# First attention of a two-layer perceiver: values weighed after every fourth step instead of after every second, and after the scores of those same steps

## The chip, the cores and the metric

The kernel runs on one core of one Trainium2 chip. The metric is the device time of one execution in microseconds (us), and of several executions the median. Engines: PE is TensorE (its weight loads are listed apart, as PEld), DVE is VectorE, ACT is ScalarE, POOL is GpSimd, SP is SyncE, which here only issues transfers.

## The reference, cut to what matters

The program is two layers of a perceiver: cross attention over a long context, a convolution mixer, a quantised feed-forward, a second cross attention, a self attention and a mixture of experts. The change touches the first cross attention alone:

```
B, S, S2, E, H = 2, 256, 4096, 256, 16;  D = E // H
q = proj(layernorm(x), Wq, bq)          # 2 x 16 heads x 256 queries x 16
k = proj(ctx, Wk, bk); v = proj(ctx, Wv, bv)   # 2 x 16 heads x 4096 keys x 16
energy = q @ k^T / sqrt(D);  energy = where(mask == 0, -1e9, energy)
attn = softmax(energy)                  # over 4096 keys
x = x + (attn @ v) @ Wo^T + bo
```

In the inputs used no entry of the mask is zero, so the kernel takes the branch without masks.

## The kernel before, in words

The attention works on 8 **groups** (`gg`, 2 batches x 4 groups of 4 heads), and each group has 32 **steps** (`KC`, 128 keys each). Two sorts of score matmuls are made of the same keys and queries:

- **Direct scores**, `scores(n)`: queries on the partitions, 2 matmuls of 512 keys each into two PSUM banks. They serve only to find the row maximum: DVE reduces the two banks (`row_tops`, L951). A unit `n` may be written once unit `n-2` is reduced (`pe.wait_ge(s_maxed, n - 1)`, L1493), since there are two pairs of banks. They run 38 units ahead of the steps (`UNITS + AHEAD`), so that they stand beside steps 0 to 217 and no longer beside steps 218 to 255.
- **Turned scores**, `turned_scores(step)`: keys on the partitions, 4 matmuls of 256 queries in two pairs. The row maximum is already taken off through extra rows of the operands. Each pair fills one bank of a **ring of 3 banks**; ACT turns it into exponentials in one of 4 buffers `PR` (`exps`, L684) and so empties it. A slot of the ring may be filled once the slot three places earlier has been emptied (`ring_free`, L1465). The order of all users of the ring is written out in `ring_slots`.
- **Weighing**, `weigh_values(step)`: 4 products of the values (32 columns each, side by side in the array) with the exponentials of the step, accumulated in the bank `PV`. They are f32, and each stands as two matmuls in the trace, 8 in a step. The buffer of a step is free for the exponentials of the fourth step after it once `pv_done` has counted it.

What else goes through the ring: in groups 0 and 1 the key projections of the second batch (`project_keys`, one piece every four steps, followed by two ACT copies, a DVE split and a POOL subtraction), in group 3 its value projections (`project_values`), the row maxima of the next group (`turn_max`), and the turning of a finished group's result (`turn_context`). Nothing is scheduled by a planner: the order on each engine is the order of the loops, and PE, ACT and DVE each have their own copy of it.

Before the change PE's loop goes over pairs of steps: turned and direct scores of the pair `m`, then the weighing of the pair `m-1`. ACT so has a whole pair's time for its exponentials before PE asks for them. At the start of a group the weighing that stands behind the first pair is still that of the group before.

Of the kernel before, what the change touches and what calls it, by code (L numbers as in the profile page):

```python
# [24 lines left out]
KC = S2 // P  # L25
# [30 lines left out]
GROUPS = B * (H // 4)  # L56
QUARTERS = 4
UNITS = 8 * QUARTERS
# [22 lines left out]

def ring_slots():

    turn = itertools.count()
# [9 lines left out]
    for gg in range(GROUPS):  # L94
        for m in range(KC // 2):
            if m == KC // 2 - 1 and gg + 1 < GROUPS:
                for pair in range(2):
                    tops[gg + 1, pair] = next(turn)
            for step in (KC * gg + 2 * m, KC * gg + 2 * m + 1):
                for pair in range(2):  # L100
                    exps[step, pair] = next(turn)
            if gg < 2 and m % 2:
                keys[1, 4 * gg + m // 4, m // 2 % 2] = next(turn)
            if gg and m == 1:
                contexts[gg - 1] = next(turn)
            if (gg == 3 and m) or (gg == 4 and m == 0):
                done = KC // 2 * (gg - 3) + m - 1
                values[1, done // 2, done % 2] = next(turn)
# [5 lines left out]


def values_after(gg, m):

    if (gg == 3 and m) or (gg == 4 and m == 0):
        return divmod(KC // 2 * (gg - 3) + m - 1, 2)
    return None  # L120


def keys_at(gg, m):

    if gg < 2 and m % 2:
        return 4 * gg + m // 4, m // 2 % 2
    return None


def build(nc, t):  # L130

    ctx = ExitStack()
    with ctx:
# [495 lines left out]
        def _(act):  # L629
# [78 lines left out]
            for gg in range(GROUPS):  # L708
                for m in range(KC // 2):
                    if m == KC // 2 - 1 and gg + 1 < GROUPS:  # L710
                        copy_tops(gg + 1)
                    exps(KC * gg + 2 * m)
                    exps(KC * gg + 2 * m + 1)
                    if keys_at(gg, m):
                        copy_keys(1, *keys_at(gg, m))
                    if gg and m == 1:
                        copy_context(gg - 1)
                    if gg and m == 0:
                        copy_weighed(gg - 1)
                    if values_after(gg, m):  # L720
                        copy_values(1, *values_after(gg, m))
# [174 lines left out]
        def _(dve):  # L896
# [150 lines left out]
            for step in range(GROUPS * KC):  # L1047
# [398 lines left out]
        def _(pe):  # L1446
# [114 lines left out]
            def attend(masked):  # L1561
# [13 lines left out]
                for gg in range(GROUPS):  # L1575
                    for m in range(KC // 2):
                        if m == KC // 2 - 1 and gg + 1 < GROUPS:
                            turn_max(gg + 1)
                        for step in (KC * gg + 2 * m, KC * gg + 2 * m + 1):
# [3 lines left out]
                        if keys_at(gg, m):  # L1583
                            project_keys(1, *keys_at(gg, m))
                        if gg and m == 1:
# [4 lines left out]
                        if values_after(gg, m):  # L1590
                            project_values(1, *values_after(gg, m))
                        if gg + 1 == GROUPS and m == KC // 4:
# [4 lines left out]
                weigh_values(GROUPS * KC - 2)  # L1597
                weigh_values(GROUPS * KC - 1)
# [471 lines left out]
```

## Time and profile before

| | |
|---|---|
| median of 3 runs | 1069.17 us (1062.98 to 1069.81) |
| the profiled execution | 1063.51 us, its span 1061.6 us |
| busy in it | PE 922.1 us (87%), DVE 601.9 us (57%), ACT 479.4 us (45%), POOL 76.2 us (7%) |
| first attention's steps | from 146.9 to 574.1 us of the span |

Shares of busy time are means over stages with different limits. The median is 5.7 us above the profiled execution; what surrounds the span is 1.9 us.

### The profile page before, as it was taken

The page shows a single profiled execution, that of the slowest core. Times are in us where ns is not written, and L with a number is a line of the kernel's source. Part 1 is how long each engine was busy: PE and PEld are TensorE (multiplying, and loading weights), DVE is VectorE, ACT ScalarE, POOL GpSimd, SP SyncE. Part 2 cuts the span into 40 slices and gives each one's busy share as a digit, 9 for nine tenths or more (in the row PEclk, how much of TensorE's full clock was granted, in tenths as well). Part 3 has the DMA queues.
Part 4 walks back from the last instruction along what each step waited for, and adds up shares of the span by engine and source line. Part 5 has one row for each costly group of instructions (what it writes and reads, how often), then busy time and mean ns, then how long its engine had stood idle before and what let it go on. Part 6 is the DMA issues. An engine that isn't in the chain of part 4 may idle for free.

```text
span 1061.6 us, 14994 instructions
## 1 busy us (share of the span) xinstructions
PE 922.1 (87%) x5928; PEld 527.9 (50%) x5928; DVE 601.9 (57%) x1064; ACT 479.4 (45%) x939; POOL 76.2 (7%) x85
## 2 busy tenths in 40 slices
PE   4367889999999999999988896249999989999878
PEld 2134544444545655555445354034656764566656
DVE  1366887778885448888723845872332227288340
ACT  1222257777775457777786330421310210677201
POOL 0131101111000000000002000300000006100000
PEclk9778999999999999999998999669999989999979
DMA  9846874665635224436235206013634450000000
GB/s 313 158 115 153 155 172 123 131 159 133 123 60 100 31 41 68 72 61 142 81 115 214 79 1 237 0 58 141 213 144 160 158 159 0 1 1 1 1 0 21
DMA packets 65555, 108.67 MB, mean 102 GB/s; under 512 B 6854, under 2 KB 40390, under 8 KB 63302
## 3 DMA queue, kind: packets, MB, share of 16 engines
q1 hardware_dynamic: 63276, 100.35, 37.0%
q10 hardware_dynamic: 2208, 7.34, 2.0%
q8 instruction: 49, 0.80, 0.4%
q14 instruction: 22, 0.18, 0.1%
HBM read 93.77 MB, written 13.89 MB: 101 GB/s over the span
## 4 chain that ended last, share of the span: by engine, by line
PE 76%; DVE 9%; ACT 6%; DMA 5%; issue 3%; SPq 1%; POOL 0%; ACTq 0%; DVEq 0%
PE psum L1547 12%; PE psum L1529 10%; PE psum L1500 9%; PE psum L1820 5%; PE psum L1791 5%; PE psum L1484 5%; PE psum L1644 4%; PE psum L1850 4%; PE psum L1474 4%; PE psum L1657 4%; PE psum L1882 3%; ACT arena L684 2%; DMA arena<-rows 2%; DMA kparts<-arena 2%; PE psum L1896 2%
## 5 line engine op out<-in xcount | busy, mean ns | idle before, releaser
L951 DVE TENSOR_REDUCE arena<-psum 128x1 f32<-128x1024 f32 x256 | 301.3, 1219 | 113.2 <-PE psum L1500 113.2
L684 ACT ACTIVATE arena<-psum 128x512 f32<-128x512 f32 x512 | 264.2, 605 | 58.5 <-PE psum L1529 57.4
L1529 PE MATMUL psum<-arena 99*128 99x256 bf16 x1024 | 160.5, 274 | 9.2 <-ACT arena L684 5.4
L1500 PE MATMUL psum<-arena 96*128 96x512 bf16 x512 | 150.6, 379 | 6.5 <-DVE arena L951 4.2
L1547 PE MATMUL psum<-arena 128*32 128x256 f32 x2048 | 136.8, 385 | 0.0
L1529 PEld LDWEIGHTS psum<-arena 99*128 99x128 bf16 x1024 | 79.3, 97 | 107.9 <-ACT arena L684 52.9
L1547 PEld LDWEIGHTS psum<-arena 128*32 128x32 f32 x2048 | 53.5, 109 | 75.4 <-ACT arena L684 36.9
L1474 PE MATMUL psum<-arena 128*128 128x512 f32 x128 | 65.5, 643 | 27.3 <-ACT arena L662 18.1
L1484 PE MATMUL psum<-arena 128*128 128x256 f32 x256 | 62.2, 385 | 0.0
L661 ACT ACTIVATE arena<-psum,arena 128x512 bf16<-128x512 f32 x32 | 22.0, 688 | 86.6 <-PE psum L1474 49.3
L1500 PEld LDWEIGHTS psum<-arena 96*128 96x128 bf16 x512 | 49.4, 98 | 23.4 <-DVE arena L951 9.1
L1820 PE MATMUL psum<-arena 128*128 128x256 f32 x256 | 55.9, 379 | 0.0
L1791 PE MATMUL psum<-arena 128*128 128x512 f32 x128 | 55.5, 593 | 0.0
L591 POOL TENSOR_TENSOR arena<-arena 128x512 bf16<-128x512 f32 x32 | 38.8, 1213 | 231.6 <-DVE arena L937 231.6
L1484 PEld LDWEIGHTS psum<-arena 128*128 128x128 f32 x256 | 47.3, 189 | 14.6 <-issue 7.5
L1474 PEld LDWEIGHTS psum<-arena 128*128 128x128 f32 x128 | 24.8, 205 | 55.7 <-issue 54.8
L1820 PEld LDWEIGHTS psum<-arena 128*128 128x128 f32 x256 | 48.3, 190 | 6.4
L667 ACT ACTIVATE arena<-psum 128x512 f32<-128x512 f32 x32 | 19.1, 597 | 67.0 <-PE psum L1484 67.0
L1644 PE MATMUL psum<-arena 128*128 128x512 f32 (+1 forms) x112 | 44.1, 551 | 3.3 <-ACT arena L743 0.9
L839 ACT ACTIVATE arena<-psum 128x512 f32<-128x512 f32 x16 | 9.6, 597 | 78.5 <-PE psum L1807 78.5
L1850 PE MATMUL psum<-arena 128*128 128x512 f32 x96 | 43.2, 610 | 0.7 <-ACT arena L741 0.7
L1258 DVE CUSTOM_DVE_ANT_0 arena<-psum,arena 128x512 f32<-128x512 f32 x32 | 22.1, 692 | 32.9 <-PE psum L1791 30.7
(231 smaller groups left out, 990.0 us busy)
## 6 DMA issues: line engine op xcount, KB each, us to landing
arena<-kparts SPq DMA_DIRECT2D x192, 128.0 KB, 5.3
kparts<-arena SPq DMA_DIRECT2D x32, 384.0 KB, 4.3
arena<-ctxT SPq DMA_DIRECT2D x18, 512.0 KB, 5.6
arena<-ctxT SPq DMA_DIRECT2D x2, 4096.0 KB, 12.8
arena<-ctx SPq DMA_DIRECT2D x2, 4096.0 KB, 14.6
arena<-mask SPq DMA_DIRECT2D x8, 1024.0 KB, 6.7
arena<-mask ACTq DMA_DIRECT2D x4, 1024.0 KB, 15.5
arena<-w1e SPq DMA_DIRECT2D x2, 2048.0 KB, 10.3
```

Source lines behind the costliest of these rows:

```text
L684: nc.scalar.activation(PR[step % 4][:, pair * CH:(pair + 1) * CH], ring_bank(slot), ACT.Exp)\
L951: nc.vector.tensor_reduce(MX[g % 2][:, col:col + 1], unit_banks(n).rearrange("p b n -> p (b n)"), AX.X, ALU.max).then_inc(s_maxed, 1)
L1474: last = nc.tensor.matmul(ring_bank(slot), WK[:, k, f * P:(f + 1) * P], CTX[n % SLOTS][:, k, :], start=(k == 0), stop=(k == CT - 1))
L1484: last = nc.tensor.matmul(ring_bank(slot)[:, v * 256:(v + 1) * 256], CTX[n % SLOTS][:, k, (2 * i + v) * P:(2 * i + v + 1) * P], WV[:, k, : ...
L1500: last = nc.tensor.matmul(out, q, KST[g % 2][0:ROWS, j, at], start=True, stop=not masked, skip_group_check=True)
L1529: last = nc.tensor.matmul(ring_heads(slot)[:, u, :], KST[gg % 2][0:KROWS, j, kc * P:(kc + 1) * P], QST[0:KROWS, G * g + j, b * S:(b + 1) * S],
L1547: last = nc.tensor.matmul(PV[32 * j:32 * (j + 1), :], V_flat[:, at:at + 32], PR[step % 4][:, j * S:(j + 1) * S], start=(kc == 0), stop=(kc ...
L1644: last = nc.tensor.matmul(out, weights[:, k, m * P:m * P + width], xs[k], start=(k == 0), stop=(k == n - 1))
L1657: last = nc.tensor.matmul(out, lhs[k], weights[:, k, :], start=(k == 0 and not biased), stop=(k == n - 1), skip_group_check=biased)
L1791: last = nc.tensor.matmul(psum[:, n % 4, :], QC[:, c, w * P:(w + 1) * P], CTXT[w // 2][:, c, n * 512:(n + 1) * 512], start=(c == 0), stop= ...
L1820: last = nc.tensor.matmul(psum[:, 6, 0:256], PT1[:, k * P:(k + 1) * P], CTXK[w // 2][:, k, :], start=(k == 0), stop=(k == KC - 1))
L1850: last = nc.tensor.matmul(psum[:, bank, :], HTF[:, c, i * P:(i + 1) * P], WQKV[which][:, c, half * HALF:(half + 1) * HALF], start=(c == 0) ...
```

## The change

PE's loop goes over runs of four steps. The turned and direct scores of the four steps come first, then the weighing of those same four steps. One piece of the key projections stands in each run of groups 0 and 1, between scores and weighing; it was in every second pair. The value projections come two pieces at a time, after the weighing of each run of group 3; before there was one in each pair, ending in group 4. The row maxima of the next group are turned at the start of its last run (step 28, before: step 30). The result of a group is copied by ACT ahead of the first exponentials of the next group, and turned after the first four steps' scores. After the last step nothing is left to weigh. ACT and DVE follow the same order; the key split of a piece stands on DVE behind the second reduction of the next run. No instruction is added or removed, no buffer, bank or ring slot is added.

```diff
+RUN = 4
+RUNS = KC // RUN
+def steps_of(gg, m):
+    return range(KC * gg + RUN * m, KC * gg + RUN * (m + 1))
...
@@ ACT
-                for m in range(KC // 2):
-                    if m == KC // 2 - 1 and gg + 1 < GROUPS:
+                for m in range(RUNS):
+                    if m == RUNS - 1 and gg + 1 < GROUPS:
                         copy_tops(gg + 1)
-                    exps(KC * gg + 2 * m)
-                    exps(KC * gg + 2 * m + 1)
...
                     if gg and m == 0:
                         copy_weighed(gg - 1)
+                    for step in steps_of(gg, m):
+                        exps(step)
+                    if gg < 2:
+                        copy_keys(1, 4 * gg + m // 2, m % 2)
+                    if gg and m == 0:
+                        copy_context(gg - 1)
+                    if gg == 3:
+                        for i in range(2):
+                            copy_values(1, m, i)
@@ DVE
-                if k % 2 == 1 and step >= 3:
-                    before = divmod(step // 2 - 1, KC // 2)
-                    if keys_at(*before):
-                        split_keys(1, *keys_at(*before))
+                if k % RUN == 1 and 0 < step // RUN <= 2 * RUNS:
+                    piece = step // RUN - 1
+                    split_keys(1, piece // 2, piece % 2)
@@ PE
-                        for step in (KC * gg + 2 * m, KC * gg + 2 * m + 1):
+                        for step in steps_of(gg, m):
                             turned_scores(step, masked)
                             if step + UNITS + AHEAD < GROUPS * UNITS:
                                 scores(step + UNITS + AHEAD, masked)
-                        if keys_at(gg, m):
-                            project_keys(1, *keys_at(gg, m))
-                        if gg and m == 1:
+                        if gg < 2:
+                            project_keys(1, 4 * gg + m // 2, m % 2)
+                        if gg and m == 0:
                             turn_context(gg - 1)
-                        if gg or m:
-                            weigh_values(KC * gg + 2 * m - 2)
-                            weigh_values(KC * gg + 2 * m - 1)
-                        if values_after(gg, m):
-                            project_values(1, *values_after(gg, m))
+                        for step in steps_of(gg, m):
+                            weigh_values(step)
+                        if gg == 3:
+                            for i in range(2):
+                                project_values(1, m, i)
...
-                weigh_values(GROUPS * KC - 2)
-                weigh_values(GROUPS * KC - 1)
                 turn_context(GROUPS - 1)
```

**PE, two pairs of steps in a middle group, before.** L1529 is turned scores, L1500 direct scores, L1547 weighing.

```order
L1529 MATMUL psum<-arena 128x256 x4
L1500 MATMUL psum<-arena 128x512 x2
L1529 MATMUL psum<-arena 128x256 x4
L1500 MATMUL psum<-arena 128x512 x2
L1547 MATMUL psum<-arena 32x256 x8
L1529 MATMUL psum<-arena 128x256 x4
L1500 MATMUL psum<-arena 128x512 x2
L1529 MATMUL psum<-arena 128x256 x4
L1500 MATMUL psum<-arena 128x512 x2
L1547 MATMUL psum<-arena 32x256 x8
```

**The same four steps after the change.** Here L1522 is turned scores, L1493 direct scores, L1540 weighing.

```order
L1522 MATMUL psum<-arena 128x256 x4
L1493 MATMUL psum<-arena 128x512 x2
L1522 MATMUL psum<-arena 128x256 x4
L1493 MATMUL psum<-arena 128x512 x2
L1522 MATMUL psum<-arena 128x256 x4
L1493 MATMUL psum<-arena 128x512 x2
L1522 MATMUL psum<-arena 128x256 x4
L1493 MATMUL psum<-arena 128x512 x2
L1540 MATMUL psum<-arena 32x256 x16
```

Four units of direct scores now follow one another without a weighing between the second and the third, and the weighings of two pairs have become one block.

**PE after the change, from step 216, where the direct scores end.** L1507 is the turning of the row maxima for group 7.

```order
L1493 MATMUL psum<-arena 128x512 x2
L1522 MATMUL psum<-arena 128x256 x4
L1493 MATMUL psum<-arena 128x512 x2
L1522 MATMUL psum<-arena 128x256 x8
L1540 MATMUL psum<-arena 32x256 x16
L1507 MATMUL psum<-arena 3x128 x8
L1522 MATMUL psum<-arena 128x256 x16
L1540 MATMUL psum<-arena 32x256 x16
```

Without direct scores between them, the turned scores of four steps, eight slots of the ring, now stand in one piece; before there were four slots and then a weighing.

**PE in group 3, before**, a pair of steps with its value projection (L1484).

```order
L1529 MATMUL psum<-arena 128x256 x4
L1500 MATMUL psum<-arena 128x512 x2
L1547 MATMUL psum<-arena 32x256 x8
L1484 MATMUL psum<-arena 128x256 x4
L1529 MATMUL psum<-arena 128x256 x4
```

After the change the weighing of 16 is followed by a value projection of 8 in a row, once in four steps.

## Rows read from the trace of the kernel before

**Rows 1.** The page: the chain that ended last, by engine.

```profile
PE 76%; DVE 9%; ACT 6%; DMA 5%; issue 3%; SPq 1%; POOL 0%; ACTq 0%; DVEq 0%
```

**Rows 2.** Timeline, one pair of group 4: start, duration in us, engine, line.

```profile
426.33 0.61 PE L1529 MATMUL psum<-arena 99*128 99x256 bf16 x4
...
426.76 2.06 ACT L684 ACTIVATE arena<-psum 128x512 f32<-128x512 f32 x4 [0.78 <-PE psum L1529]
426.77 0.60 PE L1500 MATMUL psum<-arena 96*128 96x512 bf16 x2
...
427.41 2.36 DVE L951 TENSOR_REDUCE arena<-psum 128x1 f32<-128x1024 f32 x2 [0.49 <-PE psum L1500]
...
427.65 0.60 PE L1500 MATMUL psum<-arena 96*128 96x512 bf16 x2
...
428.17 1.07 PE L1547 MATMUL psum<-arena 128*32 128x256 f32 x16
...
429.18 0.61 PE L1529 MATMUL psum<-arena 99*128 99x256 bf16 x4
```

**Rows 3.** Timeline, step 0: the one place with four steps unbroken.

```profile
148.17 4.03 ACT L684 ACTIVATE arena<-psum 128x512 f32<-128x512 f32 x8
...
149.69 3.49 DVE L951 TENSOR_REDUCE arena<-psum 128x1 f32<-128x1024 f32 x3 [0.47 <-PE psum L1500]
...
150.03 0.60 PE L1500 MATMUL psum<-arena 96*128 96x512 bf16 x2
...
151.01 0.60 PE L1500 MATMUL psum<-arena 96*128 96x512 bf16 x2
...
153.25 1.07 PE L1547 MATMUL psum<-arena 128*32 128x256 f32 x16
```

**Rows 4.** Chain ahead of the steps: direct scores held by a reduction.

```profile
120.16 1.23 DVE arena L951
...
121.44 0.60 PE psum L1500 x2
```

**Rows 5.** Timeline, the last two pairs of group 7, without direct scores.

```profile
570.68 0.83 PE L1529 MATMUL psum<-arena 99*128 99x256 bf16 x6
571.11 2.06 ACT L684 ACTIVATE arena<-psum 128x512 f32<-128x512 f32 x4 [0.34 <-PE psum L1529]
...
571.76 0.39 PE L1529 MATMUL psum<-arena 99*128 99x256 bf16 x2 [0.25 <-ACT arena L684]
...
572.08 1.93 PE L1547 MATMUL psum<-arena 128*32 128x256 f32 x32
```

**Rows 6.** Timeline, a pair of group 3 with a value projection (L1484).

```profile
337.01 0.60 PE L1529 MATMUL psum<-arena 99*128 99x256 bf16 x4
...
339.10 1.07 PE L1547 MATMUL psum<-arena 128*32 128x256 f32 x16
...
340.10 1.99 PE L1484 MATMUL psum<-arena 128*128 128x256 f32 x8
...
341.93 0.49 PE L1529 MATMUL psum<-arena 99*128 99x256 bf16 x3
```

**Rows 7.** Timeline, the last pair of group 4, from the turning of the maxima.

```profile
437.63 0.61 PE L1514 MATMUL psum<-arena 128*3 128x128 bf16 x8
...
438.17 0.92 PE L1529 MATMUL psum<-arena 99*128 99x256 bf16 x4
...
439.15 2.06 ACT L684 ACTIVATE arena<-psum 128x512 f32<-128x512 f32 x4
...
441.56 0.61 PE L1529 MATMUL psum<-arena 99*128 99x256 bf16 x4
```

**Rows 8.** Windows: length, busy us of PE, PEld, DVE, ACT, POOL; PEclk; DMA.

```profile
80.00:88.00 8.00, 2.64 (x3) 1.17 (x4) 0.00 (x0) 0.00 (x0) 0.00 (x0) 0.59 0.90 224
...
314.48:400.69 86.21, 84.50 (x649) 49.76 (x645) 44.24 (x45) 47.43 (x94) 0.00 (x0) 1.00 0.33 57
...
528.01:574.06 46.05, 41.17 (x464) 19.92 (x460) 12.89 (x13) 38.90 (x77) 0.00 (x0) 1.00 0.31 112
```

More of the change, by code:

```diff
@@ L94, in ring_slots @@
     for gg in range(GROUPS):
-        for m in range(KC // 2):
-            if m == KC // 2 - 1 and gg + 1 < GROUPS:
+        for m in range(RUNS):
+            if m == RUNS - 1 and gg + 1 < GROUPS:
                 for pair in range(2):
                     tops[gg + 1, pair] = next(turn)
-            for step in (KC * gg + 2 * m, KC * gg + 2 * m + 1):
+            for step in steps_of(gg, m):
                 for pair in range(2):
                     exps[step, pair] = next(turn)
-            if gg < 2 and m % 2:
-                keys[1, 4 * gg + m // 4, m // 2 % 2] = next(turn)
-            if gg and m == 1:
+            if gg < 2:
+                keys[1, 4 * gg + m // 2, m % 2] = next(turn)
+            if gg and m == 0:
                 contexts[gg - 1] = next(turn)
-            if (gg == 3 and m) or (gg == 4 and m == 0):
-                done = KC // 2 * (gg - 3) + m - 1
-                values[1, done // 2, done % 2] = next(turn)
+            if gg == 3:
+                for i in range(2):
+                    values[1, m, i] = next(turn)
     contexts[GROUPS - 1] = next(turn)
@@ L113 @@
 KEY_AT, VALUE_AT, EXP_AT, TOP_AT, CONTEXT_AT = ring_slots()
[L116 to L127, printed above, removed]
 def build(nc, t):
@@ L708, in _ @@
             for gg in range(GROUPS):
-                for m in range(KC // 2):
-                    if m == KC // 2 - 1 and gg + 1 < GROUPS:
+                for m in range(RUNS):
+                    if m == RUNS - 1 and gg + 1 < GROUPS:
                         copy_tops(gg + 1)
-                    exps(KC * gg + 2 * m)
-                    exps(KC * gg + 2 * m + 1)
-                    if keys_at(gg, m):
-                        copy_keys(1, *keys_at(gg, m))
-                    if gg and m == 1:
-                        copy_context(gg - 1)
                     if gg and m == 0:
                         copy_weighed(gg - 1)
-                    if values_after(gg, m):
-                        copy_values(1, *values_after(gg, m))
+                    for step in steps_of(gg, m):
[7 more added lines that the diff above has]
+                            copy_values(1, m, i)
             copy_weighed(GROUPS - 1)
@@ L1575, in attend @@
                 for gg in range(GROUPS):
-                    for m in range(KC // 2):
-                        if m == KC // 2 - 1 and gg + 1 < GROUPS:
+                    for m in range(RUNS):
+                        if m == RUNS - 1 and gg + 1 < GROUPS:
                             turn_max(gg + 1)
-                        for step in (KC * gg + 2 * m, KC * gg + 2 * m + 1):
+                        for step in steps_of(gg, m):
                             turned_scores(step, masked)
@@ L1582, in attend @@
                                 scores(step + UNITS + AHEAD, masked)
-                        if keys_at(gg, m):
-                            project_keys(1, *keys_at(gg, m))
-                        if gg and m == 1:
+                        if gg < 2:
+                            project_keys(1, 4 * gg + m // 2, m % 2)
+                        if gg and m == 0:
                             turn_context(gg - 1)
-                        if gg or m:
-                            weigh_values(KC * gg + 2 * m - 2)
-                            weigh_values(KC * gg + 2 * m - 1)
-                        if values_after(gg, m):
-                            project_values(1, *values_after(gg, m))
-                        if gg + 1 == GROUPS and m == KC // 4:
+                        for step in steps_of(gg, m):
+                            weigh_values(step)
+                        if gg == 3:
+                            for i in range(2):
+                                project_values(1, m, i)
+                        if gg + 1 == GROUPS and m == RUNS // 2:
                             pe.wait_ge(on["w_summed"], 2)
```

## The prediction

> **What bounds the kernel now.** I read the chain that ended last first: PE holds 76% of it [rows 1]. Then the timeline inside the attention, since only its order changes. In a plain pair (two steps, group 4) I count from its first turned scores at 426.33 [rows 2]: ACT starts its exponentials at +0.43, the direct scores of the two steps start at +0.44 and +1.32 (a step of turned and direct scores is 0.88), DVE starts the first reduction at +1.08, the weighing starts at +1.84, and the next pair at +2.85. No idle time stands before a matmul on PE: the pair is PE's. ACT works 2.06 of the 2.85 us and DVE 2.36; both wait for PE. The reader is to see two more things in these rows. First, PE's hand-overs: from the last direct scores to the weighing 0.52 us pass, where from direct scores to turned scores it is 0.44, and the weighing of two steps needs 1.01 us until the next matmul, though two more steps joined on to a block add only 0.86 (1.93 for 32 matmuls [rows 5] less 1.07 for 16 [rows 2]). Second, DVE's slack exists only because of the weighing: a reduction is 1.23 long [rows 4], a second one starts 1.14 after the first (2.36 for two [rows 2]), and that is more than the 0.88 in which PE makes a unit.
>
> **What the change removes.** Half of the hand-overs. A run of four steps without any wait has its last direct scores at 1.32 + 2 x 0.88 = 3.08, its weighing at 3.60, and the next run at 3.60 + 1.01 + 0.86 = 5.47, against 2 x 2.85 = 5.70: 0.23 us saved.
>
> **What it adds: DVE's wait.** Four units now follow one another with two pairs of banks. The first reduction runs from 1.08 to 2.30, the second from 2.22 to 3.44. PE wants to write the third unit at 0.44 + 2 x 0.88 = 2.20. A held unit starts 0.05 after the reduction that held it (120.16 + 1.23 = 121.39, start at 121.44 [rows 4]), so at 2.35. Turned scores follow at 2.79, and the fourth unit wants to start at 3.23 but is held until 3.44 + 0.05 = 3.49. Then the weighing is at 4.01 and the next run at 4.01 + 1.87 = 5.88, **+0.18 us a run against before**. The kernel before has one such place, step 0 to 3: units start at 150.03 and 151.01, 0.98 apart and not 0.88, and the latter just behind the end of the reduction begun at 149.69 [rows 3]. Queued behind the held direct scores are the next turned scores, for which ACT waits, and the weighing; nobody else is on the path. DVE starts the third and fourth reductions at 3.36 and 4.50 and ends at about 5.7, before the next run's second unit, so no debt is carried. In groups 0 and 1 the key split comes behind the second reduction, about 1.2 us, but the key projection gives the next run 1.7 us more. I cost it at nothing; without that cover it would hold the next run's first unit by under 1 us.
>
> **ACT and the ring in such a run.** Eight exponentials in a row take 4.03, that is one every 0.48, the last about 0.67 long [rows 3]. The eighth starts at 0.43 + 7 x 0.48 = 3.79 and ends near 4.46; its weighing, the fourth of the block, is due at 4.01 + 3 x 0.43 = 5.30. So following the same steps' scores costs no wait. The tightest slot is the eighth: its predecessor by three ends near 3.0, and PE is there at 2.79 + 0.22 = 3.01. It lies 0.2 us ahead of DVE's hold, which covers small delays. The four `PR` buffers are free, since the weighing of a run is over before the next run's first exponential.
>
> 39 runs are plain ones with four units (groups 0 to 6 without group 3, without the first run of groups 0 and 4, the last run of each group and the last two of group 6): 39 x 0.18 = **+7.0 us**.
>
> **Step 0.** Scores and keys as before up to the weighing at 153.25 [rows 3], then four steps weighed instead of two: **+0.9**.
>
> **The last runs of groups 0, 1, 2, 4, 5.** The turning of the maxima takes 0.54 up to the turned scores (437.63 to 438.17), and ACT begins the exponentials 0.98 behind these and not 0.43; the pair takes 3.39 [rows 7], 0.54 above a plain one. After, the same two delays fall on a run: following them through the ring the fourth unit starts at 3.80, the weighing at 4.32, in all 0.76 above 5.88, against 0.99 above 5.70 before: 5 x -0.05 = **-0.2**. Turning the context costs 0.22 in both.
>
> **Group 3.** A pair with values takes 4.92 (337.01 to 341.93) [rows 6]. The weighing starts at +2.09 and not +1.84, since ACT copies values ahead of the exponentials and the ring waits for it; the projection stands 1.00 behind the weighing and takes 1.83 to the next turned scores. After, ACT's lateness (0.25) disappears behind DVE's hold, and one hand-over falls away: 4.01 + 1.00 + 0.86 + 1.83 + 1.73 = 9.43 for four steps. Eight of them, the maxima (some 0.9), the context and the first run of group 4 (5.88 and its context) make 82.7, against 86.21 for the same stretch [rows 8]: **-3.5**.
>
> **Without direct scores.** A pair has its fourth slot held until the first exponential is over (571.76, +1.08), weighs at +1.40 and takes 1.40 + 1.01 = 2.41 [rows 5]. After, slots four to eight are each held, one every 0.49: the eighth fills at 1.08 + 4 x 0.49 = 3.04, the weighing is at 3.36, the run takes 5.23 against 4.82. Nine runs: 9 x 0.41 = +3.7. The run from step 216 gains 0.1, and at the end the block of four steps (1.93 [rows 5]), two of which are a debt of earlier pairs, is gone: -0.9. Together **+2.7**.
>
> **Sum:** 7.0 + 0.9 - 0.2 - 3.5 + 2.7 = **+6.9 us**. The profiled execution would go from 1063.5 to 1070.4. It is 5.7 below the median of its kernel, within the spread of the three runs (1062.98 to 1069.81); on the median the sum gives 1076. One per cent, 10.7 us, is about what a measurement of this kernel can tell from no change.
>
> What comes after the attention keeps its place relative to its end: the loads of weights wait for the weighing of group 6, now counted earlier before the end, and for the weights' quantisation, some 2 us later relative to the end but still over when it comes.
>
> **Rivals.** *No wait on DVE appears* (the reductions are quicker in a row, or PE's slack hides them): every one of the 54 runs with four units gains 0.42 on my sum, 6.9 - 22.7 = -16, **1053 us**. For it: every idle row of DVE before names PE. Against it: rows 3 show the hold with four steps in a row. 0.08.
>
> *The ring of three slots holds as well*: each held slot makes its exponentials later, and the fourth unit then waits for PE's own turned scores, not for DVE. The price is that of group 3, where late exponentials move the weighing by 0.25 [rows 6]; on the 54 runs +13.5 us, **1090 us**. It decides when the fifth exponential ends over 0.2 us later than 3.0, so that the cover of DVE's hold is used up. For it: the eight exponentials lengthen from 0.60 to 0.67 when they stand in a row [rows 3]. Against it: in those same rows the fourth step's unit still followed DVE. 0.22.
>
> *The clock falls.* Over all stages of the attention 1.00 was granted, the last stage too, where PE stood idle for 4.9 of 46.05 us in gaps of some tenths [rows 8]. The change puts gaps of 0.15 and 0.26 into each run. At 80 to 88 us, behind a long idle stretch, the granted clock was 0.59 on average, a mix of 2.4 and 1.2 GHz; a twentieth of the attention at 1.2 GHz would be some 20 us, **1095 us**. 0.03.
>
> The Trainium skill, TensorE: Matmul & The Clock Gate, section A second HAM failure mode: psum-queue depth-cycling, describes the same thing as a failure of kernels whose PE pauses briefly between groups of matmuls while it cycles through PSUM banks: the clock swings between its two levels. By that rule the change is harmful. The trace so far does not agree: the last stage pauses in this way and kept the full clock.
>
> *The change does not do what it says*, or other pieces undo it: what the scores lose, group 3 and the hand-overs give back twice over, some -5 us, 1064: part of my range, 0.07.
>
> **How the numbers follow.** The forecast, between +3 and +11 us by 0.15 us more or less in half of the runs, has 0.60. With the rivals: faster by over 1% 0.08, slower by over 1% 0.25 (the ring, the clock), within 1% 0.67. The range of 8 in 10 takes the forecast, the weak form and half of the ring's case: 1064 to 1086.
>
> **What would show it.** In the profile after: plain runs of four steps every 5.88 us (5.47: no hold; 6.1 and more: the ring); PE's direct scores with idle time before them put down to DVE; DVE's wait for PE in one piece of about 1.2 us a run; group 3's runs at 9.4; the last runs at 5.2. I am wrong if the third unit's start is not bound by the first reduction, or if turned scores rather than direct ones show the idle time where direct scores run.

## The result, and the profile after

The changed kernel takes 1076.18 us in the median of 8 executions (1071.21 to 1082.21), the kernel before beside it 1066.55 us (8 executions, 1062.98 to 1073.46). The ratio is **1.0087, 95% interval 1.0053 to 1.012**. Repeated later beside more executions of the kernel before it was 1.0051 (1.0019 to 1.0084). So the change makes the kernel slower, by 0.9% here (the interval reaches 1.2%) and by 0.5% in the repetition, some 5 to 10 us. The profiled execution took 1077.34 us, its span is 1075.5 us.

The page of the changed kernel, the chain that ended last by engine, and two of the costliest groups (their last part is the idle time before them with its releaser):

```profile
PE 67%; DVE 18%; ACT 6%; DMA 4%; issue 3%; SPq 1%; POOL 0%; ACTq 0%; DVEq 0%
...
L945 DVE TENSOR_REDUCE arena<-psum 128x1 f32<-128x1024 f32 x256 | 299.1, 1218 | 127.0 <-PE psum L1493 127.0
...
L1493 PEld LDWEIGHTS psum<-arena 96*128 96x128 bf16 x512 | 42.5, 99 | 44.5 <-DVE arena L945 30.0
```

The same weight loads on the page of the kernel before:

```profile
L1500 PEld LDWEIGHTS psum<-arena 96*128 96x128 bf16 x512 | 49.4, 98 | 23.4 <-DVE arena L951 9.1
```

Against [rows 1] DVE's share of the chain has doubled from 9 to 18% and PE's has fallen from 76 to 67%, while the reductions themselves are the same. The weight loads of the direct scores now wait 30.0 us for DVE, where they waited 9.1.

A plain run of four steps in group 4, in the timeline of the changed kernel (start, busy us, engine, line; L1522 turned scores, L1493 direct scores, L1540 weighing, L677 exponentials, L945 reductions), to be held against [rows 2], where two steps take 2.85:

```profile
425.87 0.61 PE L1522 MATMUL psum<-arena 99*128 99x256 bf16 x4
...
426.30 4.03 ACT L677 ACTIVATE arena<-psum 128x512 f32<-128x512 f32 x8 [1.87 <-PE psum L1522]
426.32 0.60 PE L1493 MATMUL psum<-arena 96*128 96x512 bf16 x2
...
426.95 4.62 DVE L945 TENSOR_REDUCE arena<-psum 128x1 f32<-128x1024 f32 x4 [1.28 <-PE psum L1493]
...
427.19 0.60 PE L1493 MATMUL psum<-arena 96*128 96x512 bf16 x2
...
427.93 0.11 PEld L1522 LDWEIGHTS psum<-arena 99*128 99x128 bf16 x2 [0.20 <-ACT arena L677]
428.23 0.11 PEld L1493 LDWEIGHTS psum<-arena 96*128 96x128 bf16 x2 [0.19 <-DVE arena L945]
428.24 0.61 PE L1493 MATMUL psum<-arena 96*128 96x512 bf16 x2
...
429.36 0.11 PEld L1493 LDWEIGHTS psum<-arena 96*128 96x128 bf16 x2 [0.34 <-DVE arena L945]
429.37 0.61 PE L1493 MATMUL psum<-arena 96*128 96x512 bf16 x2
...
429.90 1.93 PE L1540 MATMUL psum<-arena 128*32 128x256 f32 x32
...
431.77 0.61 PE L1522 MATMUL psum<-arena 99*128 99x256 bf16 x4
```

From 425.87 to 431.77 the run takes **5.90 us**; 5.88 was forecast. The third unit starts at +2.37 (forecast 2.35), the fourth at +3.50 (3.49), the weighing at +4.03 (4.01). The weights of both units (428.23 and 429.36) waited for DVE, and both waits end just behind a reduction. DVE's four reductions go from 426.95 to 431.57, 4.62 us without a pause, and then DVE waits 1.28 us. The chain of waits through this run puts DVE where it binds:

```profile
426.48 0.45 PE psum L1493 x2
...
426.95 2.37 DVE arena L945 x2
...
429.97 1.86 PE psum L1540 x32
```

From the end of the first two direct scores the end is set by two reductions in a row (2.37) and not by the two steps of scores that PE makes meanwhile. What the chain doesn't show is the row at 427.93: the second pair of turned scores of the third step waited for ACT. It lies ahead of DVE's hold, which covers it.

In group 3 the reader is to see that one block of 16 matmuls of the value projections (L1477) takes the place of two of 8, against [rows 6]:

```profile
334.20 0.60 PE L1522 MATMUL psum<-arena 99*128 99x256 bf16 x4
...
335.27 2.36 DVE L945 TENSOR_REDUCE arena<-psum 128x1 f32<-128x1024 f32 x2 [5.04 <-PE psum L1493]
...
337.49 0.11 PEld L1522 LDWEIGHTS psum<-arena 99*128 99x128 bf16 x2 [0.21 <-ACT arena L677]
...
337.73 0.60 PE L1493 MATMUL psum<-arena 96*128 96x512 bf16 x2
...
340.12 3.72 PE L1477 MATMUL psum<-arena 128*128 128x256 f32 x16
...
343.68 0.60 PE L1522 MATMUL psum<-arena 99*128 99x256 bf16 x4
```

A run takes 9.48 us (two pairs before: 9.85). The hold here is not DVE's. The fourth unit starts at 337.73, 0.10 behind the end of the two reductions at 337.63, but its weights did not wait for DVE; the turned scores before it waited for ACT (337.49), as those of the second and third step did (335.53 and 336.51). DVE would have let the unit start some 0.05 us earlier.

Without direct scores, against [rows 5], eight pairs of turned scores go through three slots, and ACT paces them, one every 0.49 us:

```profile
568.49 0.83 PE L1522 MATMUL psum<-arena 99*128 99x256 bf16 x6
568.91 4.03 ACT L677 ACTIVATE arena<-psum 128x512 f32<-128x512 f32 x8 [1.20 <-PE psum L1522]
...
569.57 2.35 PE L1522 MATMUL psum<-arena 99*128 99x256 bf16 x10 [0.25 <-ACT arena L677]
...
571.85 1.93 PE L1540 MATMUL psum<-arena 128*32 128x256 f32 x32
```

Two such runs follow each other every 5.23 us, as in the window of 552.80 below (two pairs before: 4.82).

Windows of the changed kernel (span, its length, busy time of PE, PEld, DVE, ACT, POOL, then the granted clock as a share of 2.4 GHz, DMA share, GB/s): step 0's run, the middle of the attention, and the first two runs of group 7:

```profile
150.75:160.41 9.66, 9.01 (x60) 4.56 (x60) 5.02 (x5) 6.68 (x11) 0.00 (x0) 0.82 0.32 118
270.00:540.00 270.00, 266.18 (x2413) 140.24 (x2412) 192.38 (x202) 178.15 (x357) 2.32 (x2) 1.00 0.41 80
545.41:552.80 7.39, 6.66 (x54) 2.63 (x51) 2.56 (x4) 4.60 (x10) 0.00 (x0) 0.77 0.81 276
552.80:558.03 5.23, 4.59 (x52) 2.01 (x49) 2.62 (x2) 4.03 (x8) 0.00 (x0) 1.00 0.45 190
```

Within these steps the clock was full (2.4 GHz) for the 270 us in the middle and fell twice, to 1.2 GHz for 3.4 us of the trace each: in step 0's run and in the first run of group 7.

The sum for the steps of the first attention, from the first turned scores to the last weighing (146.91 to 574.01 before, 427.1 us; 150.75 to 589.69 after, 438.9 us):

| part | before | after | difference | forecast |
|---|---|---|---|---|
| 39 plain runs (in groups 0 and 1 with 1.72 more for the keys, in both kernels) | 5.70 each | 5.90 each | +7.7 | +7.0 |
| step 0's run | 7.34 | 9.66 | +2.3 | +0.9 |
| last runs of groups 0, 1, 2, 4, 5 | | | -0.1 | -0.2 |
| group 3 and first run of group 4 | 86.21 | 83.66 | -2.6 | -3.5 |
| from step 216 to the end | 51.26 | 55.73 | +4.5 | +2.7 |
| all | 427.1 | 438.9 | +11.8 | +6.9 |

What comes after the attention took 485.9 us after and 487.6 before, and the steps began 3.8 us later, though nothing ahead of them was changed. These two parts are not the order's.

### The profile page after: what moved, and what is told of

Same layout as the page of the kernel before. It is cut to its first block, busy times and chain, and to the rows that moved or that the text cites. A ratio compares the mean times of both kernels' runs of the same rounds, so it can differ in the third digit from the quotient of the medians.

```text
span 1075.5 us, 14993 instructions
## 1 busy us (share of the span) xinstructions
PE 932.4 (87%) x5927; PEld 529.4 (49%) x5928; DVE 599.5 (56%) x1064; ACT 473.6 (44%) x939; POOL 76.3 (7%) x85
## 3 DMA queue, kind: packets, MB, share of 16 engines
q10 hardware_dynamic: 2208, 7.34, 2.0%
## 4 chain that ended last, share of the span: by engine, by line
PE 67%; DVE 18%; ACT 6%; DMA 4%; issue 3%; SPq 1%; POOL 0%; ACTq 0%; DVEq 0%
PE psum L1540 11%; DVE arena L945 9%; PE psum L1493 7%; PE psum L1811 5%; PE psum L1782 5%; PE psum L1477 5%; PE psum L1522 5%; PE psum L1635 4%; PE psum L1841 4%; PE psum L1467 4%; PE psum L1648 4%; PE psum L1873 3%; ACT arena L677 3%; DMA arena<-rows 2%; PE psum L1887 1%
## 5 line engine op out<-in xcount | busy, mean ns | idle before, releaser
L945 DVE TENSOR_REDUCE arena<-psum 128x1 f32<-128x1024 f32 x256 | 299.1, 1218 | 127.0 <-PE psum L1493 127.0
L677 ACT ACTIVATE arena<-psum 128x512 f32<-128x512 f32 x512 | 257.8, 628 | 66.8 <-PE psum L1522 66.6
L1522 PE MATMUL psum<-arena 99*128 99x256 bf16 x1024 | 170.4, 276 | 10.0 <-ACT arena L677 3.2
L1493 PE MATMUL psum<-arena 96*128 96x512 bf16 x512 | 153.5, 386 | 9.2 <-DVE arena L945 4.2
L1522 PEld LDWEIGHTS psum<-arena 99*128 99x128 bf16 x1024 | 77.8, 98 | 116.0 <-ACT arena L677 43.2
L1540 PE MATMUL psum<-arena 128*32 128x256 f32 x2048 | 125.4, 386 | 0.0
L1540 PEld LDWEIGHTS psum<-arena 128*32 128x32 f32 x2048 | 60.4, 110 | 62.3 <-issue 15.8
L1493 PEld LDWEIGHTS psum<-arena 96*128 96x128 bf16 x512 | 42.5, 99 | 44.5 <-DVE arena L945 30.0
L1477 PE MATMUL psum<-arena 128*128 128x256 f32 x256 | 61.7, 390 | 0.0
L1477 PEld LDWEIGHTS psum<-arena 128*128 128x128 f32 x256 | 49.5, 196 | 12.6 <-issue 4.8
L1467 PEld LDWEIGHTS psum<-arena 128*128 128x128 f32 x128 | 25.8, 207 | 55.2 <-issue 52.5
L1811 PEld LDWEIGHTS psum<-arena 128*128 128x128 f32 x256 | 48.3, 190 | 6.4
L660 ACT ACTIVATE arena<-psum 128x512 f32<-128x512 f32 x32 | 19.1, 597 | 68.0 <-PE psum L1477 68.0
L833 ACT ACTIVATE arena<-psum 128x512 f32<-128x512 f32 x16 | 9.6, 597 | 78.5 <-PE psum L1798 78.5
L1648 PE MATMUL psum<-arena 128*128 128x256 f32 (+1 forms) x160 | 38.8, 411 | 2.0 <-ACT arena L735 1.5
```

Source lines behind the costliest of these rows:

```text
L677: nc.scalar.activation(PR[step % 4][:, pair * CH:(pair + 1) * CH], ring_bank(slot), ACT.Exp)\
L945: nc.vector.tensor_reduce(MX[g % 2][:, col:col + 1], unit_banks(n).rearrange("p b n -> p (b n)"), AX.X, ALU.max).then_inc(s_maxed, 1)
L1467: last = nc.tensor.matmul(ring_bank(slot), WK[:, k, f * P:(f + 1) * P], CTX[n % SLOTS][:, k, :], start=(k == 0), stop=(k == CT - 1))
L1477: last = nc.tensor.matmul(ring_bank(slot)[:, v * 256:(v + 1) * 256], CTX[n % SLOTS][:, k, (2 * i + v) * P:(2 * i + v + 1) * P], WV[:, k, : ...
L1493: last = nc.tensor.matmul(out, q, KST[g % 2][0:ROWS, j, at], start=True, stop=not masked, skip_group_check=True)
L1522: last = nc.tensor.matmul(ring_heads(slot)[:, u, :], KST[gg % 2][0:KROWS, j, kc * P:(kc + 1) * P], QST[0:KROWS, G * g + j, b * S:(b + 1) * S],
```

## The experiments

The theory was that DVE's hold of the third and fourth unit sets the run; the rival, that the ring's hold behind the exponentials does so as well. Two kernels shorten one of the two each.

**The changed kernel with half of each reduction** (DVE reads 256 of the 512 columns of each bank):

```diff
-                nc.vector.tensor_reduce(MX[g % 2][:, col:col + 1], unit_banks(n).rearrange("p b n -> p (b n)"),
-                                        AX.X, ALU.max).then_inc(s_maxed, 1)
+                nc.vector.tensor_reduce(MX[g % 2][:, col:col + 1], unit_banks(n)[:, :, 0:CH // 2],
+                                        AX.XY, ALU.max).then_inc(s_maxed, 1)
```

> The changed kernel, with each reduction of direct scores reading 256 of the 512 columns of both banks: half of the keys are left out of the row maximum. Theory (the third and fourth units of a run are held by DVE's two reductions, 0.15 + 0.26 us): the first reduction is over by about 1.8 us after the run's start, no unit is held, a plain run takes 5.47 us and not 5.90, in all 54 runs with four units; about 1053 us, 23 us less than the changed kernel and 13 less than the kernel before. Rival (the hold is the ring's or a cost of PE's own order): a plain run stays at 5.9 us and the time at 1076.

Measured: 1067.01 us (10 executions), ratio 0.9993 (0.9968 to 1.0017). A reduction takes 0.69 us, and the whole loss is gone, but the gain of 1053 is not there. Its timeline shows why:

```profile
429.43 0.61 PE L1522 MATMUL psum<-arena 99*128 99x256 bf16 x4
...
431.19 0.70 PE L1522 MATMUL psum<-arena 99*128 99x256 bf16 x4
...
431.49 0.12 PEld L1522 LDWEIGHTS psum<-arena 99*128 99x128 bf16 x2 [0.20 <-ACT arena L677]
...
431.72 0.60 PE L1493 MATMUL psum<-arena 96*128 96x512 bf16 x2
...
432.16 0.71 PE L1522 MATMUL psum<-arena 99*128 99x256 bf16 x4
...
432.70 0.60 PE L1493 MATMUL psum<-arena 96*128 96x512 bf16 x2
...
433.23 1.93 PE L1540 MATMUL psum<-arena 128*32 128x256 f32 x32
```

The turned scores of the third and fourth step last 0.70 and 0.71 instead of 0.61, since their second pair (the sixth and the eighth slot) waits for ACT; the weighing starts at +3.80, not 3.60. A plain run takes 5.66 us: shorter reductions give back 0.24 of 0.43. Group 3's runs stay at 9.48. My expectation for this kernel missed.

**The kernel before with the same half reductions**, as a control:

> The control: the kernel before with the same halved reductions (half of the keys left out of the row maximum). Theory: a pair is PE's alone, it stays at 2.85 us and the time within 0.3% of the kernel before, save a few us ahead of step 0, where the direct scores already wait for DVE. Rival (shorter reductions help by themselves, through ports or shared waits): pairs get shorter as runs do.

Measured: 1065.93 us, ratio 0.998 (0.9957 to 1.0004); a pair still takes 2.85 us. Before the change DVE bound nothing in the pairs.

**The changed kernel with exponentials of half width** from step 4 on (ACT reads 256 of 512 columns; the rest of `PR` keeps old values):

```diff
-                    nc.scalar.activation(PR[step % 4][:, pair * CH:(pair + 1) * CH], ring_bank(slot), ACT.Exp)\
+                    width = CH if step < 4 else CH // 2
+                    nc.scalar.activation(PR[step % 4][:, pair * CH:pair * CH + width], ring_bank(slot)[:, 0:width], ACT.Exp)\
```

> The changed kernel, with each exponential after the first four steps covering 256 of 512 columns: half of the weights are stale. ACT is about twice as fast. Theory: plain runs with direct scores stay at 5.90 us, since DVE holds them; only the runs without direct scores, which the ring holds, fall from 5.23 to about 3.75 (4 x 0.44 + 0.1 + 1.87); some 13 us less than the changed kernel, about 1063. Rival (the ring holds the runs with direct scores as well): these fall too, to 5.7 or below.

Measured: 1060.03 us, one execution. Plain runs take 5.90 us as before (425.93 to 431.82):

```profile
427.01 4.62 DVE L946 TENSOR_REDUCE arena<-psum 128x1 f32<-128x1024 f32 x4 [1.28 <-PE psum L1494]
...
429.42 0.61 PE L1494 MATMUL psum<-arena 96*128 96x512 bf16 x2
```

No matmul waits for ACT before the weighing (the third and fourth units, at 428.29 and 429.42, wait for DVE), and the run hasn't moved: with full exponentials too, DVE alone sets it. Group 3's runs take 9.44 (9.48). Without direct scores a run takes 4.20 us, not the 3.75 I expected: eight half exponentials last 2.40, one every 0.29, still more than the 0.22 in which PE makes a pair of turned scores, so the slots are held all the same. The clock didn't fall near step 0 here, and the first run took 8.21 us, 0.87 above before's 7.34.

**Both halves at once:**

> The changed kernel with both halvings: reductions of half the columns (half of the keys out of the row maximum) and exponentials of half the columns after step 3 (half of the weights stale). Theory after the first runs (DVE holds a run for 0.43 us; with DVE out of the way the ring holds it for 0.19, at the second pairs of the third and fourth steps): with both out of the way a plain run takes what PE needs, 5.47 us; with one alone it took 5.66 or 5.90. Rival (what is left at 5.66 is a cost of PE's own): 5.66.

Measured: 1039.8 us, one execution. A plain run, from one weighing to the next, with nothing held between:

```profile
405.80 1.93 PE L1541 MATMUL psum<-arena 128*32 128x256 f32 x32
...
411.25 0.42 PE L1541 MATMUL psum<-arena 128*32 128x256 f32 x4
```

The run takes 5.46 us; the forecast's figure for a run without any wait was 5.47. Group 3's runs take 9.05. So the four values for a plain run are 5.90 as it is, 5.90 with quick exponentials, 5.66 with quick reductions, 5.46 with both: DVE's hold is worth 0.44 and the ring's 0.20, and they lie one behind the other on the same matmuls, so that only the larger counts. In group 3 either half alone gives little (9.44 with the exponentials, 9.48 with the reductions) and both give 0.43: there the ring sets the run and DVE's hold lies 0.04 behind it. The last runs of the groups are like that too: 6.21 us as they are and with quick reductions, 6.20 with quick exponentials, 5.78 with both.

For the other questions I wrote the order of all steps as one list from which PE, ACT, DVE and the ring take theirs; with pairs throughout it is the order of the kernel before. Each kernel changes one line of what makes the list.

**Pairs whose values follow their own scores** (the weighing of pair `m` behind the scores of pair `m`):

```diff
-OWN_PAIRS = False
+OWN_PAIRS = True
```

> The kernel before with one part of the change: pairs of two steps stay, but the weighing follows the scores of its own pair (and the value projection its own pair, the finished group's copy comes ahead of the first exponentials). As many hand-overs as before. Theory: the fourth exponential of a pair ends at 0.43 + 3 x 0.48 + 0.61 = 2.48 and the second weighing wants to start at 2.27, so it is held for about 0.25 us: a pair takes 3.10 us and not 2.85, a pair without direct scores 3.1 and not 2.41; some 93 x 0.25 + 19 x 0.7 = 36 us more than before, about 1102. In runs of four the same exponentials had 0.8 us to spare. Rival (the weighing's place costs nothing, only the number of hand-overs does): 2.85 us, the time of before.

Measured: 1105.69 us, one execution, 465.0 us for the stage. A pair in group 4:

```profile
431.90 0.61 PE L1602 MATMUL psum<-arena 99*128 99x256 bf16 x4
...
433.75 1.34 PE L1620 MATMUL psum<-arena 128*32 128x256 f32 x16
434.45 0.16 PEld L1620 LDWEIGHTS psum<-arena 128*32 128x32 f32 x8 [0.54 <-ACT arena L761]
...
435.02 0.39 PE L1602 MATMUL psum<-arena 99*128 99x256 bf16 x2
```

The second half of the weighing waits for the fourth exponential (1.34 where 1.07 is needed), and the pair takes 3.12 us instead of 2.85. Following one's own scores costs 0.27 a pair in runs of two and nothing in runs of four, as forecast for the latter.

**Runs of four only towards the end, pairs before.** The line says step 216; since the pair before it is still to be weighed there, steps 216 to 219 run as two pairs, and runs of four begin with step 220:

```diff
-    return False
+    return KC * gg + 2 * m >= 216
```

> The kernel before, in runs of four from step 216 on only, where direct scores end. Theory: each run without direct scores takes 5.23 us where two pairs take 4.82, since the exponentials stand still while four steps are weighed and the ring of three slots lets PE run no further ahead; with 0.9 us back at the end, the stretch from step 216 to the last weighing is about 3 us longer than before. Rival (the loss of the changed kernel in its last stage was the clock and other chance): no longer than before by over 1 us.

Measured: 1075.11 us, one execution; from step 216 to the end 57.29 us against 51.26 before, 6.0 more and not 3. Runs without direct scores take 5.23, as expected, and group 7 as a whole takes 2.5 more than before. Steps 216 to 219, where the order goes over from one form to the other, cost another 2.0 (7.28 against 5.25). The rest is the clock: it fell in the run from step 220, which took 7.36 and not 5.78, and its block of weighing lasted 3.30 where it otherwise lasts 1.93:

```profile
537.00:540.50 3.50, 3.47 (x34) 1.49 (x34) 0.00 (x0) 1.44 (x3) 0.00 (x0) 0.52 0.00 0
```

**The opposite, runs of four up to step 215 and pairs after** (`< 216`):

> The changed kernel's runs of four up to step 216, then the kernel before's pairs (and in between nothing else changed; the weighing trails by a pair again). Theory: the stretch from step 216 to the last weighing falls from 54.1 (55.7 with the clock's fall) to about 51.3, and PE's clock does not fall in it, since it did not in any kernel with pairs there. Rival (the fall comes from how the execution lies in time): it falls here as well.

Measured: 1069.26 us, one execution; from step 216 on 50.38 us, where the changed kernel needs 55.73, and the clock stayed full (1.00 from 530 to 581 us). The kernel before needs 51.26, but it has the weighing of an earlier pair to do in that stretch, some 0.9 us, which this one and the changed one have not. So the loss of the last stage can be had back by its order alone: 5.35 us, of which 1.6 are the clock's fall and 3.7 the form of the runs.

**Runs of four in group 3 alone,** values in the old place behind the weighing, then **the same with the values of the run before behind the second step:**

```diff
-    return False
+    return gg == 3 and m
```

> The kernel before, in runs of four in group 3 only, as the change has them: both value projections of a chunk behind the weighing. Theory: DVE's hold costs 0.43 there, but a hand-over and ACT's late ring slots (0.25 a pair) fall away: 9.48 us a run against 9.85; about 3 us less than before in that stretch, 0.3% in all. Rival (the gain in group 3 hangs on runs of four in the groups around it): no gain.

Measured: 1065.37 us, ratio 0.998 (0.9962 to 0.9998); group 3 with the first run of group 4 takes 83.47 us against 86.21. A run takes 9.48, as forecast, but by the ring's hold and not by DVE's, as the rows of group 3 above show.

```diff
-MIDDLE = False
+MIDDLE = True
```

> As the one before, but with the value projections of the previous chunk in the middle of the run, between the second and the third unit of direct scores. Theory: DVE reduces during the projections, no unit is held, and only one ring slot of 0.23 us is: about 1.75 + 3.46 + 1.98 + 0.08 + 1.87 = 9.15 us a run against 9.48 and 9.85: 5 to 6 us less than before, 0.5%. It is the version that I expect to beat both kernels. Rival (the copies of the values then hold the ring for more than they free): 9.5 or more.

Measured: 1065.07 us, ratio 0.9976 (0.9953 to 0.9999); the same stretch takes 80.49 us, 5.7 less than before. A run:

```profile
340.43 0.60 PE L1602 MATMUL psum<-arena 99*128 99x256 bf16 x4
...
345.47 2.35 DVE L1024 TENSOR_REDUCE arena<-psum 128x1 f32<-128x1024 f32 x2 [1.62 <-PE psum L1573]
...
346.14 3.62 PE L1557 MATMUL psum<-arena 128*128 128x256 f32 x16
...
349.60 0.60 PE L1602 MATMUL psum<-arena 99*128 99x256 bf16 x4
...
350.04 0.60 PE L1573 MATMUL psum<-arena 96*128 96x512 bf16 x2
```

With 3.62 us of projections between the second and the third unit the two reductions are over long before the third is wanted (347.82 against 350.04). 9.17 us a run are left (340.43 to 349.60), 0.31 less than in the changed kernel. The two medians differ by less than either interval, so the 3.0 us between the two placements stand on the traces alone.

**The last of these, and from step 218 on each step alone:** scores of a step, then the weighing of the step two before. What makes the list has a branch for it, which this line turns on:

```diff
-SINGLY = 10000
+SINGLY = 218
```

> The best version that the runs point to: pairs as before, group 3 in runs of four with the value projections in the middle (9.17 us a run against 9.85), and from step 218 on, without direct scores, one step's turned scores and then one weighing, two steps back. There a pair is held by the ring for 0.41 us, and one more hand-over costs 0.23: I expect 2 x (0.44 + 0.09 + 0.43 + 0.14) = 2.20 us against 2.41, 4 us less over 19 pairs, besides the 5.7 of group 3: 10 us less than before in the attention, about 1057 against 1067. Rival (hand-overs cost more when they come after every step, or the exponentials come too late for them): 2.4 or more, and 1061.

Measured: **1058.78 us** (10 executions, 1056.9 to 1063.5), **ratio 0.9929 (0.9902 to 0.9956)**. It beats both kernels. Two steps without direct scores:

```profile
551.22 0.61 PE L1609 MATMUL psum<-arena 99*128 99x256 bf16 x4
...
552.34 0.61 PE L1609 MATMUL psum<-arena 99*128 99x256 bf16 x4
...
553.45 0.39 PE L1609 MATMUL psum<-arena 99*128 99x256 bf16 x2
```

They take 2.23 us here, against 2.41 in pairs [rows 5] and 2.61 in runs of four. There are twice as many hand-overs as in pairs, but each weighing (0.64 us, at 551.76 and 552.88) is time in which ACT empties slots. The last stage takes 47.74 us (-3.5), group 3 again -5.7; the sum of 9.2 is the whole difference in the stage (417.86 against 427.10).

**The changed kernel and the kernel before, each once more,** to see what an execution does by itself:

> The changed kernel once more. Theory: its plain runs take 5.90 us again, to 0.01; the falls of PE's clock ahead of step 0 and in the last stage, and the 3.8 us by which step 0 came later, are of one execution and change from run to run. Rival (the change brings the clock's falls): they stand at the same places.

> The kernel before once more: is its first profile a typical one? Theory: the same stage times to 0.02 us, but the fall of PE's clock near step 0 (1.5 to 3 us), which the first profile lacked and which kernels with the same code there showed, may appear; none in the last stage. Rival (the first profile is typical): step 0 to 3 takes 7.34 again.

Measured: 1073.91 us, ratio 1.0051 (1.0019 to 1.0084), and 1067.5 us, ratio 0.9994 (0.9968 to 1.002). The changed kernel's runs are the same to 0.01 us as in its first profile, its stage takes 438.98 us, and the clock fell again at both places. The second half of that expectation so missed: the rival, that the falls stand at the same places, holds for this kernel, in two profiles of two. The kernel before shows in this profile a fall near step 0; the window of 147 to 152 us of its span:

```profile
147.00:152.00 5.00, 3.17 (x20) 1.55 (x20) 3.44 (x4) 3.10 (x5) 0.00 (x0) 0.83 1.05 372
```

In its first profile the same window had a clock of 1.00. Its first run took 7.99 us here instead of 7.34, 0.65 more where I had expected 1.5 to 3. Between 145 and 165 us of the span the granted clock was below 1.00 (0.83 or 0.91) in 11 of the 14 profiles, and full in the other three, the first profile of the kernel before among them. So the fall near step 0 isn't the change's.

## Why the prediction was right, and where a term was off

- **DVE's wait, 39 x 0.18 = +7.0: right.** 5.90 a run against 5.88, +7.7 in all. The mechanism is shown by the two half kernels: with quick exponentials a plain run doesn't move, with quick reductions the loss goes.
- **The precedent for it, rows 3, was misread.** I took the 0.98 us between the units at 150.03 and 151.01 for DVE's hold. The rows around them say otherwise:

```profile
149.05 0.60 PE L1500 MATMUL psum<-arena 96*128 96x512 bf16 x2
...
150.78 0.11 PEld L1529 LDWEIGHTS psum<-arena 99*128 99x128 bf16 x2 [0.21 <-ACT arena L684]
```

  The unit at 150.03 is 0.98 behind the one before it as well, and the reduction that it needs had been over since 149.22 (begun at 148.00). In front of both units the turned scores waited 0.21 for ACT. With halved reductions two units of a plain run are again 0.98 apart (431.72 and 432.70). So rows 3 show the hold of the ring, 0.10 a step, and were no evidence for DVE's hold, nor against the rival of the ring. DVE's hold follows from the length of a reduction and the pace of PE, and that part was right.
- **The saved hand-overs, a run of 5.47 without waits: right.** 5.46 with both halves.
- **The ring in a plain run: its place was named incompletely.** I named the eighth slot as the tightest, 0.2 us ahead of DVE's hold. By the same figures the sixth is as tight: PE is there at 2 x 0.88 + 0.22 = 1.98, and the third exponential ends at 0.43 + 2 x 0.48 + 0.60 = 1.99. In the changed kernel the sixth is held (427.93) and the eighth is not, since DVE's hold of the third unit has made PE late for it; DVE's holds cover it, so it cost nothing, as forecast. With quick reductions both are held, by 0.10 each. But the rival without DVE's wait was priced as if nothing stood behind DVE: 0.42 a run and 1053 us. The ring would have taken 0.20 of it; the half reductions gave 1067. Removing the named bound showed the next one. The rival that the ring holds as well came true in the runs of group 3, but at no price of its own, since DVE's hold ends within 0.05 us of it.
- **Following the same steps' scores costs ACT nothing: right** in runs of four (5.90 in both kernels), and it would have been wrong in pairs (+0.27 each).
- **Step 0, +0.9: right as a term**, 0.87 in the profile without a fall of the clock. The 2.3 in the profile of the changed kernel hold 1.4 us of a fall that the kernel before has in other executions too.
- **Last runs, -0.2: measured -0.1.**
- **Group 3, -3.5: measured -2.6, with the wait named wrongly.** I had ACT's lateness disappear behind DVE's hold. It is the other way round: the ring sets the run, and quick reductions leave it at 9.48. That the figure was near (9.43) is luck, since the two holds end at almost the same time. Besides, the two runs with the maxima are together 1.2 and not 0.9 longer, and the first of group 4 takes 6.42 and not some 6.1 (6.42 with quick reductions too, 6.17 with quick exponentials, so this is ACT's as well).
- **Without direct scores, +2.7: measured +4.5.** Nine runs at 5.23 against 4.82, as forecast, are +2.8 with the end. The other 1.6 are a fall of the clock in the first run of group 7: 7.39 us, against 5.76 for the same run with the same instructions in the kernel with half reductions, where the clock stayed full.
- **The clock as a rival: it came true once, and small.** I expected that the pauses of 0.15 and 0.26 in each run, if they did harm, would do it everywhere (1095 us). The 270 us of the middle, with 0.34 before the last held loads of each plain run, kept 1.00. Only in the last stage, where five pairs of weights in a run wait 0.38 us or more for ACT, it went to 1.2 GHz for 3.4 us, in three of the four profiles with full exponentials and runs of four there, and in none of those with pairs or single steps there. In the changed kernel and its repetition it fell in the first run of group 7, where the turning of the context waits another 0.38, in the kernel with fours only at the end one run earlier, where no context is turned; in the one with half reductions it did not fall. That the pauses bring the fall is likely by this count but not shown. The Trainium skill, TensorE: Matmul & The Clock Gate, section A second HAM failure mode: psum-queue depth-cycling, says that short pauses between groups of matmuls that cycle through PSUM banks make the clock swing back and forth. The plain runs don't agree with it (1.00 over 270 us); the last stage agrees at most in part, with one fall in a profile, worth 1.6 us, and no swinging, and the kernel with half reductions shows that the same order can go without.

Without the two falls the stage would be +8.8 against +6.9. The forecast, 1076.0, and the median, 1076.18, agree more closely than the terms do: the sum was 1.9 us short in the order's own cost, and the median of the kernel before, on which it was set, was 2.6 above the one measured beside the result. With the clock's part the medians differ by 9.6 and not 6.9; that this 2.7 and the 2.6 nearly cancel is luck. The measured median lies inside the range, and the change, 0.9%, inside the 1% that the largest chance was given to, though its interval reaches beyond.

Open is what decides in which run of the last stage the clock falls, and whether it falls at all. A kernel that keeps the order and changes only PE's pauses there was not tried.

## What to carry to other kernels

Longer runs of one kind of matmul save hand-overs, here 0.23 us for every two that go, but they take away what the other kind gave: time for the engine behind to empty its banks. Before merging, compare the producer's pitch in an unbroken row with the consumer's (0.88 against 1.14 here, and 0.22 against 0.49 without direct scores) and the number of buffers between; where the consumer is slower, split rather than merge, and put unrelated work of the producer between the units. And when a hold is found, look for the second one that it covers, because that is what a removal will meet.

## What the runs showed of the hardware that I had not expected

- Eight exponentials in a row keep a pitch of 0.48 to 0.49 us though each lasts 0.60 to 0.67, and half-width ones, each 0.38 long, a pitch of 0.29: they overlap, and the pitch, not the length, sets the ring.
- The clock fell in stages that the change doesn't touch, in some executions and not in others: the first turned scores of kernels with the same instructions ahead of them came between 146.8 and 152.6 us of the span, and what follows the attention took 485.7 to 491.1. This is as large as the change, and the reason why the stage's own time (438.94 and 438.98 in two profiles of the changed kernel, 427.10 and 427.76 in two of the one before) says more about the order than one execution's total.
- A fall of 3.4 us cost 0.65 us in the first run of the kernel before (7.99 against 7.34), 1.4 in that of the changed kernel (9.66 against 8.21) and 1.6 in group 7, where the weighing of four steps took 3.57 us, from 549.30, instead of 1.93.
